# Half of the pair products of a DLRM interaction with the batch on partitions, summed along the free dimension by ScalarE and VectorE; batch in quarters of 128

## The reference

```python
e = jnp.stack([tbl_0[ids[:, 0]], ..., tbl_31[ids[:, 31]]], axis=1)   # (512, 32, 64)
xi, xj = e[:, idx_i, :], e[:, idx_j, :]                              # the 496 pairs
z = jnp.sum(jnp.einsum('bpd,pde->bpe', xi, W) * xj, axis=-1)         # (512, 496)
h = jnp.concatenate([z, dense_ctx], axis=1)                          # (512, 512)
h = jnp.maximum(h @ W_top1 + b_top1, 0.0)                            # 512 -> 512
h = jnp.maximum(h @ W_top2 + b_top2, 0.0)                            # 512 -> 256
y = h @ W_top3                                                       # 256 -> 1
```

## Time and profile before

| | us |
|---|---|
| median of three timed runs | 253.86 (253.63 to 254.2) |
| profiled execution, its own time | 254.16 |
| its span, first to last instruction | 252.4 |
| TensorE busy | 223.3 |
| VectorE busy | 158.3 |
| GpSimd busy (issuing gathers) | 121.6 |
| ScalarE busy | 14.9 |

### The profile page before, as it was taken

How to read it: one execution, slowest core, us unless ns; L and a number is a source line. 1 busy time by engine, 2 the same in 40 slices (tenths; PEclk the granted TensorE clock), 3 DMA queues, 4 the chain that set the end, 5 groups by cost and what they waited for, 6 DMA issues and landing times.

```text
span 252.4 us, 3921 instructions
## 1 busy us (share of the span) xinstructions
PE 223.3 (88%) x1652; PEld 126.8 (50%) x1652; DVE 158.3 (63%) x157; ACT 14.9 (6%) x35; POOL 121.6 (48%) x134
## 2 busy tenths in 40 slices
PE   0026569999999999999969999999999999999996
PEld 0013245555555665655545655656555555653441
DVE  3002327777778788788845777777888878771122
ACT  2010001000000000000021000000000000000110
POOL 5777777777777777777777777500000000000000
PEclk9999999999999999999999999999999999999999
DMA  6999931111111111111111111100000000000000
GB/s 185 374 366 367 372 73 29 26 26 29 26 29 27 28 26 29 27 27 31 26 26 29 26 28 26 26 4 0 3 0 3 0 0 3 0 3 0 0 0 0
DMA packets 10002, 14.51 MB, mean 57 GB/s; under 512 B 3569, under 2 KB 3569, under 8 KB 9858
## 3 DMA queue, kind: packets, MB, share of 16 engines
q1 hardware_dynamic: 5890, 10.07, 11.6%
q0 software_dynamic: 4096, 4.20, 8.8%
HBM read 14.26 MB, written 0.00 MB: 57 GB/s over the span
## 4 chain that ended last, share of the span: by engine, by line
PE 84%; POOL 7%; DMA 3%; issue 3%; ACT 1%; DVE 1%; DVEq 0%
PE left L262 47%; PE zsum L274 24%; POOL rows L166 7%; PE left L282 6%; PE turned L245 4%; PE left L324 3%; DMA rows<-tbl_dram,ids 3%; DMA ids<-ids_dram 1%; PE turned L329 1%; ACT xt L178 1%; DVE z L213 0%; DVE xt L233 0%; DVE prod L202 0%; DVEq L198 0%
## 5 line engine op out<-in xcount | busy, mean ns | idle before, releaser
L202 DVE TENSOR_TENSOR prod<-left,xt 128x1024 f32<-128x1024 f32 x112 | 130.8, 1219 | 37.2 <-PE left L262 37.2
L166 POOL DMA_INDIRECT rows<-tbl_dram,ids x128 | 120.9, 945 | 40.3 <-issue 38.7
L262 PE MATMUL left<-xt,w 64*128 64x256 f32 x1024 | 130.9, 399 | 2.9 <-ACT xt L178 2.4
L262 PEld LDWEIGHTS left<-xt,w 64*128 64x128 f32 x1024 | 97.2, 192 | 41.3 <-issue 14.3
L274 PE MATMUL zsum<-prod,selector 128*32 128x512 f32 x512 | 61.6, 598 | 0.3 <-DVE z L213 0.3
L245 PE MATMUL turned<-ident,rows 128*128 128x128 f32 x64 | 15.5, 328 | 23.6 <-DMA rows<-tbl_dram,ids 23.0
L204 DVE TENSOR_TENSOR prod<-left,xt 128x512 f32<-128x512 f32 x16 | 11.0, 688 | 33.1 <-PE left L262 33.1
L274 PEld LDWEIGHTS zsum<-prod,selector 128*32 128x32 f32 x512 | 13.6, 109 | 30.4 <-issue 23.8
L245 PEld LDWEIGHTS turned<-ident,rows 128*128 128x128 f32 x64 | 6.9, 152 | 36.8 <-DMA rows<-tbl_dram,ids 25.6
L178 ACT ACTIVATE xt<-turned 128x256 f32<-128x256 f32 x32 | 12.3, 384 | 195.8 <-PE turned L245 195.8
L282 PE MATMUL left<-z,w 128*128 128x512 f32 x32 | 14.3, 599 | 0.0
(11 more groups left out here) (11 smaller groups left out, 2.6 us busy)
## 6 DMA issues: line engine op xcount, KB each, us to landing
w<-pair_w_dram SPq DMA_DIRECT2D x32, 256.0 KB, 7.2
rows<-tbl_dram,ids POOLq DMA_INDIRECT x128, 2.4
w<-w_top_dram SPq DMA_DIRECT2D x1, 1024.0 KB
w<-w_top_dram SPq DMA_DIRECT2D x1, 512.0 KB
dense<-dense_t_dram SPq DMA_DIRECT2D x16, 2.0 KB
ids<-ids_dram SPq DMA_DIRECT2D x1, 64.0 KB, 2.0
w<-w_top_dram SPq DMA_DIRECT2D x1, 1.0 KB
b<-b_top_dram SPq DMA_DIRECT2D x1, 2.0 KB
```

The costliest lines, as they stand in the source:

```text
L166: pool.indirect_dma_start(out=rows[:, part, n, t, h, :], out_offset=None, in_=a[f"tbl_{f}"], in_offset=bass.IndirectOffsetOnAxis(ap=ids[:, ...
L202: dve.tensor_tensor(out, inp, other, ALU.mult).then_inc(prod_done, 1)
L262: mm = pe.matmul(left[:, k % LEFT_BUFS, half, i, :], w[own, u, :], xt[own, moving_of(u, half), cols(part)], start=True, stop=True)
```

## The change

The batch is worked in four parts of 128. A group is now four units (`GU`), a part has 32 groups, and the table `GROUPS` gives their order and the kind of each.

- **A COL group** works as before: batch on the free dimension, matmuls of 64x128 columns (L393), eight for a group, then a reduction by `selector` with 256 columns moving (L405). There are 16 in a part.
- **A ROW group** swaps the operands: `xt` is the stationary side and the matrices of four units move, 512 columns (L386, two matmuls for a group). The result has the batch on partitions and 16 blocks of 64 elements on the free dimension. VectorE multiplies it by the gathered `rows` as they are (L304). The 16 sums go along the free dimension. For 5 of a part's 16 ROW groups (`DVE_ROWS`) VectorE does them in one TENSOR_REDUCE (L325); for the other 11 (`ACT_ROWS`) ScalarE does them with 16 ACTIVATEs of 64 elements, each with an accumulator output into one column of `sums` (L257). The built program holds, behind each such ACTIVATE, one more ScalarE instruction that reads the accumulator out: 704 of either.
- Once in a part `sums` is transposed (L369) and copied by ScalarE into `z` (L243). `turned` and its copies are counted by one semaphore, `turn_copied`.
- In each engine's program, a transpose of `xt` stands ahead of the group that `TURN_AT` names. In ScalarE's, the copy of that transpose stands at the same group's number k, and behind it the sums of group k-4 (`behind`).
- The loads of `w` wait on SyncE until the embeddings five pairs before are gathered, and the gathers of part 2 and 3 wait until part 0 and 1 are multiplied.

```diff
-PARTS = 2
-PB = B // PARTS
-TB = PB // P
...
+GU = 4
+PARTS = BT
+PB = P
+COL, ROW = 0, 1
...
+GROUPS = [
+    (COL, units(1, 0, None) + units(2, 0, 1)),
+    (COL, units(3, 0, 1, 2, None)),
+    (ROW, units(4, 0, 1, 2, 3)),
+    (ROW, units(5, 0, 1, 2, 3)),
+    (ROW, units(6, 0, 1, 2, 3)),
...
+    (COL, units(9, 4, 5, 6, 7)),
...
+    (ROW, units(15, 0, 1, 2, 3)),
+    (COL, units(15, 8, 9, 10, 11)),
+    (ROW, units(15, 4, 5, 6, 7)),
+    (COL, units(15, 12, 13, 14, None)),
+]
...
+DVE_ROWS = [i for i in range(NROW) if i % 3 == 2]
+ACT_ROWS = [i for i in range(NROW) if i % 3 != 2]
...
-AHEAD_G = [0, 0, 0, 0, 1, 1, 1, 1, 2, 2, 2, 3, 3, 3, 3, 3]
...
+COL_BUFS = 2 * BATCH
+ACT_BUFS = 6
+DVE_BUFS = 2
+
+TURN_AT = [0, 0, 0, 1, 2, 3, 4, 6, 8, 10, 12, 15, 17, 20, 23, 26]
+EARLY = [-4, -3, -2, -1]
+Z_TURN_AT = 12
+Z_COPY_AT = BATCH + 1
...
+def turn_before(part, n):
+    at = EARLY[n] if part and n < len(EARLY) else TURN_AT[n]
+    return max(NG * part + at, 0)
...
+        rows = sb("rows", [P, 2, NP, 2, D])
+        xt = sb("xt", [P, 2, NP, PB])
...
+        prod_col = sb("prod_col", [P, COL_BUFS, 2, GU, PB])
+        prod_act = sb("prod_act", [P, ACT_BUFS, 16, D])
+        prod_dve = sb("prod_dve", [P, DVE_BUFS, 16, D])
...
+        sums = sb("sums", [P, PARTS, ZR, P])
...
+        turns = sorted([(turn_before(part, n), part, n) for part in range(PARTS) for n in range(NP)]
+                       + [(NG * (part + 1) + Z_TURN_AT, part, None) for part in range(PARTS)],
+                       key=lambda t: t[0])
...
-            for c in range(NC):
-                sp.dma_start(w[:, CU * c:CU * c + CU, :], a["pair_w"][c]).then_inc(w_loaded[c], 16)
+            for g in range(NG):
+                n = max(u[0] for u in GROUPS[g][1])
+                if n >= 5:
+                    sp.wait_ge(rows_loaded[0][n - 5], 32)
+                sp.dma_start(w[:, g, :, :], a["pair_w"][g]).then_inc(w_loaded[g], 16)
...
+                if part >= 2:
+                    pool.wait_ge(prod_done, NG * (part - 1))
...
         def _(act):
-            for part in range(PARTS):
-                for n in range(NP):
-                    k = NP * part + n
-                    act.wait_ge(turn_done, k + 1)
-                    act.activation(xt[:, n, cols(part)], turned[:, :PB], ACT.Copy).then_inc(x_done, 1)
+            def copy_turned(part, n):
+                act.wait_ge(turn_done, turn_number[part, n])
+                if n is None:
+                    act.activation(z[:, ZC:, cols(part)], turned[:, :ZR * PB].rearrange("p (c b) -> p c b", b=PB),
+                                   ACT.Copy).then_inc(turn_copied, 1)
+                    return
+                if part >= 2 and n == 0:
+                    act.wait_ge(prod_done, NG * (part - 1))
+                act.activation(xt[:, part % 2, n, :], turned[:, :PB], ACT.Copy).then_inc(turn_copied, 1)
+
+            def sum_rows(part, g):
+                i = ROW_AT[g]
+                k = len(ACT_ROWS) * part + ACT_ROWS.index(i)
+                act.wait_ge(prod_done, NG * part + g + 1)
+                for j in range(16):
+                    col = 16 * (i % 8) + j
+                    p = prod_act[:, k % ACT_BUFS, j, :]
+                    op = act.activation(p, p, ACT.Copy, accum_out=sums[:, part, i // 8, col:col + 1])
+                op.then_inc(act_summed, 1)
+
+            behind = 4
+            t = 0
+            for k in range(PARTS * NG + behind):
+                while t < len(turns) and turns[t][0] <= k:
+                    copy_turned(*turns[t][1:])
+                    t += 1
+                part, g = (k - behind) // NG, (k - behind) % NG
+                if part >= 0 and g in ROW_AT and ROW_AT[g] in ACT_ROWS:
+                    sum_rows(part, g)
+            while t < len(turns):
+                copy_turned(*turns[t][1:])
+                t += 1
...
+                if kind == ROW:
+                    i = ROW_AT[g]
+                    n, m = group[0]
+                    if i in ACT_ROWS:
+                        c = len(ACT_ROWS) * part + ACT_ROWS.index(i)
+                        if c >= ACT_BUFS:
+                            dve.wait_ge(act_summed, c - ACT_BUFS + 1)
+                        out = prod_act[:, c % ACT_BUFS, :, :]
+                    else:
+                        c = len(DVE_ROWS) * part + DVE_ROWS.index(i)
+                        if c >= DVE_BUFS:
+                            dve.wait_ge(dve_summed, c - DVE_BUFS + 1)
+                        out = prod_dve[:, c % DVE_BUFS, :, :]
+                    other = rows[:, part % 2, m:m + GU, :, :].rearrange("p m h d -> p (m h d)")
+                    dve.tensor_tensor(out.rearrange("p (h j) d -> p h (j d)", h=2), inp,
+                                      other.unsqueeze(1).to_broadcast([P, 2, BANK]), ALU.mult).then_inc(prod_done, 1)
                     return
...
+                c = NCOL * part + COL_AT[g]
+                if c >= COL_BUFS:
+                    dve.wait_ge(reduce_done, c - COL_BUFS + 1)
...
+            def sum_rows(part, g):
+                i = ROW_AT[g]
+                c = len(DVE_ROWS) * part + DVE_ROWS.index(i)
+                dve.wait_ge(prod_done, NG * part + g + 1)
+                dve.tensor_reduce(sums[:, part, i // 8, 16 * (i % 8):16 * (i % 8) + 16], prod_dve[:, c % DVE_BUFS, :, :],
+                                  AXIS.X, ALU.add).then_inc(dve_summed, 1)
...
+                part, g = k // NG, k % NG
+                multiply(part, g)
+                before = (k - 1) % NG
+                if k and before in ROW_AT and ROW_AT[before] in DVE_ROWS:
+                    sum_rows((k - 1) // NG, before)
+                if part and g == COLS[Z_COPY_AT]:
+                    copy_z(part - 1)
+            copy_z(PARTS - 1)
...
+            def turn(part, n):
+                number = turn_number[part, n]
+                if n is None:
+                    pe.wait_ge(act_summed, len(ACT_ROWS) * (part + 1))
+                    pe.wait_ge(dve_summed, len(DVE_ROWS) * (part + 1))
+                else:
+                    pe.wait_ge(rows_loaded[part % 2][n], 32 * (part // 2 + 1))
+                if number == 1:
                     pe.wait_ge(ident_ready, 1)
                 else:
-                    pe.wait_ge(x_done, k)
-                for t in range(TB):
-                    mm = pe.transpose(turned[:, P * t:P * t + P],
-                                      rows[:, part, n, t, :, :].rearrange("p h d -> p (h d)"), ident[:])
+                    pe.wait_ge(turn_copied, number - 1)
+                if n is None:
+                    for c in range(ZR):
+                        mm = pe.transpose(turned[:, PB * c:PB * c + PB], sums[:, part, c, :], ident[:])
...
+                kind, group = GROUPS[g]
+                pe.wait_ge(turn_copied, turn_number[part, max(u[0] for u in group)])
                 if k >= LEFT_BUFS:
                     pe.wait_ge(prod_done, k - LEFT_BUFS + 1)
-                for i in range(GU):
-                    u = GU * g + i
-                    if part == 0 and u % CU == 0:
-                        pe.wait_ge(w_loaded[u // CU], 16)
+                if part == 0:
+                    pe.wait_ge(w_loaded[g], 16)
+                if kind == ROW:
                     for half in range(2):
                         own = slice(D * half, D * half + D)
-                        mm = pe.matmul(left[:, k % LEFT_BUFS, half, i, :], w[own, u, :],
-                                       xt[own, moving_of(u, half), cols(part)], start=True, stop=True)
+                        mm = pe.matmul(left[:, k % LEFT_BUFS, half, :], xt[own, part % 2, group[0][0], :],
+                                       w[own, g, :, :], start=True, stop=True)
+                    mm.then_inc(left_done, 1)
+                    return
+                for i in range(GU):
+                    for half in range(2):
+                        own = slice(D * half, D * half + D)
+                        mm = pe.matmul(left[:, k % LEFT_BUFS, half, PB * i:PB * i + PB], w[own, g, i, :],
+                                       xt[own, part % 2, moving_of(group[i], half), :], start=True, stop=True)
...
+            def reduce(c):
+                part, q = c // NCOL, c % NCOL
+                pe.wait_ge(prod_done, NG * part + COLS[q] + 1)
+                if q == 0 and part:
+                    pe.wait_ge(z_done, part)
+                for half in range(2):
+                    for pair in range(2):
+                        s = 2 * half + pair
                         mm = pe.matmul(zsum[32 * s:32 * s + 32, :, :], selector[:, 30 - 2 * q:62 - 2 * q],
-                                       prod[:, k % PROD_BUFS, half, :, :], start=(q == 0), stop=(q == 15),
-                                       tile_position=(0, 32 * s))
...
+            while reduced < PARTS * NCOL:
+                reduce(reduced)
+                reduced += 1
+            while t < len(turns):
+                turn(*turns[t][1:])
```

(76 more changed lines are left out.)

225 lines of the change are left out of this document (100 added, 125 removed).

## The result

The changed kernel takes 309.84 us (median of four runs, 309.17 to 310.67), the kernel before 253.75 in the same comparison (253.06 to 254.2). The ratio is 1.2215, 95% interval 1.2171 to 1.2259. The profiled execution took 310.23 us. An execution can fall into a second state that is some per cent slower; of all runs in this document only two did, of the later repeat of the changed kernel (444.48 and 449.47 us).

A forecast was written before the change was run, and what follows sets the result against it. ScalarE's many short sums, in fixed order with TensorE's transposes, were to set the time: 39.4 + 4P (P = 73.9) = 335 us, plus 19.5 for the clock and 1.8 for execution over span, 356 us; range 285 to 405.

The forecast's parts named there:

- the pair overlaps itself: Rival: successive ScalarE sums and accumulator reads overlap, 0.235 us for both, total 300 us; chance 27%.
- The price of the pair: ScalarE's cost for one 64-element sum plus its accumulator read, taken as 0.31 us, the middle of the estimates.
- c: ScalarE's time for one sum with its accumulator read, forecast 0.31 us.
- S: ScalarE's time for the 16 sums and reads of one ROW group, forecast 4.96 us.
- P: Time of one of the four parts, forecast 14 G + 11 S = 73.9 us.
- G: Time of one group, set by VectorE level with TensorE, forecast 44.3/32 = 1.38 us.
- The stretches: Between successive transposes the engine with more work sets the time; 16 a part, listed as groups:sums, ScalarE's sums decide.
- looser transposes: Transposes of n = 12 to 15 and 0 to 3, left out as offsetting each other.
- The clock: After TensorE's long rests the next two groups run at 1.2 GHz, costing 4.9 us a part, 19.5 us in all.
- Weight loads bound COL groups: Rival: 16 weight loads in each COL group, one at a time, add 10 us a part to TensorE, 353 us; chance 5%.
- The free read: Rival: ScalarE's accumulator reads cost nothing, 0.155 us a pair, total 248 us, deciding below S = 2.78; chance 12%.
- What would show it: Signs in the profile: ScalarE busiest, over 200 us, TensorE waiting mostly for ScalarE, clock below full in some slices.

The follow-up runs named there:

- e1: Changed kernel with ScalarE's sums lacking their accumulator output, so without the reads; last part 45.3 us against 60.5, whole 384.29 us.
- e4: Changed kernel with the same instructions, transposes of parts 1 to 3 placed elsewhere in the order; last part 41.5 us against 60.5, whole 407.28 us.
- e2: Changed kernel with only one of the sixteen sums of each ScalarE group kept; last part 44.3 us against 60.5, whole 378.38 us.
- c1_after: Changed kernel, unaltered, run again in the conditions of the experiments; whole 436.47 us, last part 60.5 us.
- e6: Changed kernel with useless matmuls added ahead of groups 28, 8 and 3 of a part; last part 56.8 us against 60.5, whole 446.19 us.
- c2_before: Kernel before the change, unaltered, run in the conditions of the experiments; whole 395.5 us.

## Why the prediction was right in its kind and 46 us too high

The forecast was 356 us, slower, with a range of 285 to 405; the time is 309.84. The direction and the lock-step were right; the price of ScalarE's sums was not. The time fell on the first rival of the list, "the pair overlaps itself" (300 us, 27%; the prediction once calls it the second). It lies inside the range because the range was drawn to hold that rival, not because the forecast's own case came true.

- **The price of the pair, the term that was mis-sized.** Forecast c = 0.31 us, S = 4.96; measured 0.238 and 3.81. By the forecast's own formula P becomes 20 G + 9 S = 27.6 + 34.3 = 61.9 instead of 73.9, 48 us less over four parts, and the whole 39.4 + 247.6 + 19.5 + 1.8 = 308.3 us, where the profiled execution has 310.2 (how far that is luck stands below). The reason given for the middle, that the read has to follow the end of the sum, is wrong for the pitch: a read starts 0.146 us behind its sum, before that one's 0.24 us are over. The estimate from the Trainium skill (ScalarE: Activation LUTs, "What ACT_TABLE_LOAD costs"), 146 ns for the sum and 94 for the read, met both: 0.15 with the read left out (e1), 0.09 for the read. The page prices no accumulator read; the 94 takes it as an ACTIVATE of one element. I had the estimate in hand and gave it 27%.
- **The stretches.** Right, and shown by e4. Between the seventeen successive copies from 87.03 to 151.41 us of the first trace lie 3.99, 2.82, 4.27, 7.81, 2.63, 3.99, 5.81, 4.00, 3.98, 4.48, 7.81, 0.89, 3.99, 0.88, 3.99 and 3.04 us. With the list of the prediction and S = 3.81, G = 1.38, every 1:1, every 2:1 and both double sums (2:2, 3:2) come to within 0.2 us (3.81 and 7.62, plus the hand-over that I left out). The first of these rows, the second, and two around the 2:2 stretch:

```profile
87.03 0.28 ACT L248 ACTIVATE xt<-turned 128x128 f32<-128x128 f32 x1 [5.27 <-PE turned L371]
91.02 0.25 ACT L248 ACTIVATE xt<-turned 128x128 f32<-128x128 f32 x1
...
98.11 0.28 ACT L248 ACTIVATE xt<-turned 128x128 f32<-128x128 f32 x1 [3.99 <-PE turned L371]
105.92 0.26 ACT L248 ACTIVATE xt<-turned 128x128 f32<-128x128 f32 x1
```

 What was off: the 1:0 and 2:0 at its start are 2.9 us over (the clock, below); the 3:1 that holds the turning of `sums` and a reduction is 1.7 over; the looser transposes around the part's end are 3.5 under; the other stretches, from 0.2 under to 0.3 over, add 1.3. That errors of both signs nearly cancel (64.4 against 61.9) is luck. And the rule overprices the window of the last part: from e2 to c1_after it gives 61.9 + 3.7 - 44.2 = 21.4 us, measured 16.2, and from e2 to e1 50.1 - 44.2 = 5.9, measured 1.0. The looser transposes would be 3.5 of the 5 us; that they are it in this window is not shown.
- **The clock.** It falls, but not only where forecast. The forecast put a fall behind the 2:2 stretch. There TensorE rests 3.65 us ahead of group 8 in part 1 and in the last part alike, and its next four L386 take 1.13 us at 106.23 and 2.08 at 235.82. So in part 1 the granted clock stays at 1.00 behind that rest (its mean from 98 to 138 us is 1.00), and the 2:0 stretch takes 2.63 us between its copies; in parts 0, 2 and 3 it takes 4.53, 4.53 and 4.54, 1.9 more, where the forecast had 2.4. The clock also falls where none was forecast: ahead of group 3 of part 1, after a rest of 2.58 us, it goes to 0.50, the lower level, from 92 to 96 us, and costs the 2.9 us of those two stretches. The chain has the three places:

```profile
91.32 2.08 PE left L386 x4
...
106.23 1.13 PE left L386 x4
...
235.82 2.08 PE left L386 x4
```

 Over a part the granted clock is 0.85 to 0.89, where it was 9 in every slice before; e6 won 3.7 us back in the last part, where the forecast has 4.9. The rule of the Trainium skill that the clock has to be earned by activity (TensorE: Matmul & The Clock Gate, "What's actually happening") agrees with e6, where added matmuls raised the granted clock from 0.86 to 0.97.
- **G.** Right as VectorE's work: it is busy 44.15 and 44.23 us of a part, forecast 44.3, with TENSOR_REDUCE at 1.208 us against 1.16 and L304 at 1.218. The pace that it gives is a little too fast: e2 takes 1.43 us a group, not 1.38.
- **The end.** Right: three groups' sums in one go, 11.46 us, then `sums` turned and copied, then the layers as before. The chain:

```profile
270.91 11.46 ACT prod_act L257 x96
282.38 0.04 issue
282.42 0.45 PE turned L369 x2
...
283.43 13.97 PE left L412 x32
297.40 6.87 PE left L452 x16
```

- **Weight loads bound COL groups.** Refuted: the eight matmuls of a COL group (four units, two halves) take 0.89 us (at 107.36), under the 0.91 assumed.
- **The free read.** Refuted by the pair. e1 agrees with the limit that the forecast worked out for it: with S = 2.43, below 2.78, the window is only 1.0 us above e2's and the clock stays at 1.00. No run lies near the limit, so where it is exactly is not shown.
- **What would show it.** "ScalarE busiest, over 200 us" was a poor sign: it is busy 186.7, because the pair costs less than forecast (704 x 0.238 is 168, 704 x 0.31 would be 218), and TensorE is busy 236.3, since at a low clock its own work lasts longer. The waits were the good one.

That the sum with the measured S comes to 308.3 against 310.2 is luck in part. Without its 19.5 us for the clock it gives a span of 287.0; the trace has 308.4, 21.4 more. By the copies of n = 4 (they start at 19.07, 87.03, 151.41 and 217.67 us) and the end of the last sums (282.37), 1 us of that lies in the start, 6.5, 2.5, 4.4 and 7.0 in the four parts, and nothing in the end. Part 1 is taken apart above: there the clock has 2.9, hand-overs and the turning of `sums` 3.0, and the looser transposes give 3.5 back. The other parts were not taken apart, so the 19.5 us stand for more than the clock.

## What to carry to other kernels

Where two engines hand work to each other in a fixed order, count what each has to do between two successive hand-overs and add the longer of the two, stretch by stretch; the averages here (VectorE and ScalarE busy 44 to 46 us a part) hid a period of 64 to 66. If no engine is full and two appear as each other's releaser, move the hand-overs before moving work: here the same instructions in another order took 41.5 us in place of 60.5, and 78.6 in place of 95.4 to the end. Price many small instructions by their pitch back to back, not by the duration of one.

## What the runs showed of the hardware

- **Late signals beside gathers.** In the experiments a copy waited 25.52 and 27.59 us (c2_before's chain) while GpSimd issued gathers, and copies ran as usual when they were over; in the first trace TensorE worked through its gathers. The trace names no cause, and none was looked for.
- **An accumulator output is a second instruction.** It is 0.189 us long in the trace and adds 0.09 us to the pitch of a 64-element sum (0.238 with it, 0.152 without).
- **The clock behind rests.** The same rest, 3.65 us ahead of group 8, was followed by matmuls at the lower level of the clock, 1.2 GHz, in the last part and at the full 2.4 GHz in part 1 of one trace (four L386 in 2.08 and in 1.13 us). Matmuls without use in the rests raised the granted clock from 0.86 to 0.97 and made the last part 3.7 us shorter (e6).
